# FP6 rounding in a macaron block: ScalarE makes the rounding constant and the half unit from the scaled values, VectorE drops its AND and, for activations, its OR

## What is computed

```python
def _nearest_on_grid(x, grid):                 # grid: all fp6 e2m3 values
    idx = jnp.clip(jnp.searchsorted(grid, x), 0, grid.shape[0] - 1)
    idx_lo = jnp.maximum(idx - 1, 0)
    v_hi, v_lo = grid[idx], grid[idx_lo]
    return jnp.where(jnp.abs(x - v_lo) <= jnp.abs(x - v_hi), v_lo, v_hi)

def _mx_quantize(t, eps=1e-30):                # blocks of 32 along a row
    blocks = t.reshape(rows, K // 32, 32)
    scales = jnp.maximum(jnp.max(jnp.abs(blocks), axis=-1) / 7.5, eps)
    return _nearest_on_grid(blocks / scales[..., None], _GRID), scales

# both the normed activations x2 and the weight w2 are quantized
out = xd @ wd.T + bias                          # xd = xq * xs, wd = wq * ws
x = x + 0.5 * _L1_ffn_ref(_layernorm(x), weight, bias)   # twice in the chain
```

## Time and profile before

| what | value |
|---|---|
| median of 3 runs | 2559.42 us (2553.13 to 2559.54) |
| span of the profiled execution | 2554.8 us (its page gives no other time of it; the median lies 4.6 us above) |
| instructions | 38679 |
| TensorE matmul busy | 2128.9 us, 83% of the span |
| VectorE busy | 1539.1 us, 60% |
| ScalarE busy | 970.2 us, 38% |
| GpSimd busy | 314.8 us, 12% |
| granted TensorE clock, mean | 0.903 of full |
| fourth stage (first `linear`) | about 1424 to 1644 us of the span |
| last stage (second `linear`) | about 2429 us to the end |

### The profile page before, as it was taken

One profiled execution on the slowest core, in us unless ns is written; L12 is line 12 of the kernel. 1 busy time (PEld: TensorE's weight loads), 2 busy tenths in 40 slices (PEclk: granted clock), 3 DMA queues, 4 the chain that ended last, 5 costly groups with the idle time before them and its releaser, 6 DMA issues.

```text
span 2554.8 us, 38679 instructions
## 1 busy us (share of the span) xinstructions
PE 2128.9 (83%) x12842; PEld 1592.0 (62%) x12842; DVE 1539.1 (60%) x4444; ACT 970.2 (38%) x1961; POOL 314.8 (12%) x298
## 2 busy tenths in 40 slices
PE   4589999957999956899999456578998998999846
PEld 2478888856788935788888335434445545555435
DVE  7744343446455577434343598576876776778287
ACT  4122232322333342232323334235556556555532
POOL 4320000031000044100000432311002002000000
PEclk8699999978999978999999657579999999999956
DMA  8110111020000031110110310422422422422001
GB/s 260 43 64 24 31 30 31 26 64 26 1 1 1 1 116 58 51 31 27 29 30 26 91 44 25 73 46 58 51 28 51 74 29 54 72 29 27 2 25 50
DMA packets 84036, 114.84 MB, mean 45 GB/s; under 512 B 12212, under 2 KB 73816, under 8 KB 80728
## 3 DMA queue, kind: packets, MB, share of 16 engines
q1 hardware_dynamic: 77416, 94.80, 17.0%
q0 software_dynamic: 6432, 17.57, 2.2%
HBM read 69.16 MB, written 43.17 MB: 44 GB/s over the span
## 4 chain that ended last, share of the span: by engine, by line
PE 61%; DVE 26%; ACT 5%; issue 4%; DMA 2%; POOL 2%; DVEq 0%; ACTq 0%; SPq 0%; POOLq 0%
PE psum L775 10%; PE psum L777 10%; PE psum L776 10%; PE psum L126 5%; PE psum L2298 4%; PE psum L128 4%; PE psum L127 4%; DVE mt L2186 3%; PE psum L2277 3%; PE psum L862 3%; DVE m L2174 2%; PE psum L2257 2%; DVE stats L160 2%; DVE m L2183 2%; DVE xn L185 2%
## 5 line engine op out<-in xcount | busy, mean ns | idle before, releaser
L2137 ACT ACTIVATE pt<-psum 128x512 f32<-128x512 f32 (+3 forms) x768 | 333.9, 492 | 274.9 <-DVE psum L2212 180.1
L740 DVE SCALAR_TENSOR_TENSOR h<-psum,xg,sg 128x128 f32<-128x128 f32 x592 | 166.7, 344 | 415.6 <-PE psum L862 415.6
L556 ACT ACTIVATE sg<-psum 128x512 f32<-128x512 f32 x180 | 107.7, 598 | 575.1 <-PE psum L777 575.1
L775 PE MATMUL psum<-w_hi,xt_hi 128*128 (+1 forms) x720 | 285.6, 397 | 33.7 <-DVE xt_lo L705 33.7
L776 PE MATMUL psum<-w_lo,xt_hi 128*128 (+1 forms) x720 | 283.8, 394 | 0.0
L777 PE MATMUL psum<-w_hi,xt_lo 128*128 (+1 forms) x720 | 283.7, 394 | 0.0
L2257 PE MATMUL psum<-ks,qs 96*128 96x512 bf16 (+3 forms) x768 | 235.5, 347 | 36.0 <-DVE m L2174 10.2
L2277 PE MATMUL psum<-qs,ks 99*128 99x512 bf16 (+3 forms) x768 | 239.0, 334 | 24.4 <-ACT pt L2137 18.8
L775 PE MATMUL psum<-w_hi,ht_hi 128*128 (+1 forms) x720 | 218.1, 303 | 0.2
L2186 DVE CUSTOM_DVE_ANT_0 mt<-psum,band_q 128x256 bf16<-128x256 f32 (+1 forms) x512 | 204.2, 399 | 18.3 <-PE psum L2257 8.1
L2281 PE MATMUL psum<-band,ident_r 128*128 128x256 f32 (+1 forms) x864 | 214.8, 337 | 0.0
(11 more groups left out here) (284 smaller groups left out, 4420.1 us busy)
## 6 DMA issues: line engine op xcount, KB each, us to landing
xg<-w_dram SPq DMA_DIRECT2D x54, 256.0 KB, 3.2
qk_scr<-parts SPq DMA_DIRECT2D x32, 384.0 KB, 2.5
qs<-qk_scr SPq DMA_DIRECT2D x96, 128.0 KB, 7.2
ks<-qk_scr SPq DMA_DIRECT2D x96, 128.0 KB, 7.8
xg<-rows_in SPq DMA_DIRECT2D x74, 132.0 KB, 2.1
rows_out<-yb SPq DMA_DIRECT2D x74, 128.0 KB, 1.7
x<-x_dram SPq DMA_DIRECT2D x4, 1024.0 KB, 8.6
out_dram<-x SPq DMA_DIRECT2D x4, 1024.0 KB, 4.5
```

The source lines that it names most:

```text
L740: ins = dve.scalar_tensor_tensor(out=h[i % 2][:, e, :], in0=u[:, e, :], scalar=xg[j % XSLOT][:, at:at + 1], in1=sg[i % 2][:, e, :], op0=AL ...
L775: pe.matmul(out, a[0], b[0], start=first, stop=False)
L2137: act.activation(pt[n % NPT][:, 0:q1 - q0], st_bank(n)[:, 0:q1 - q0], ACT.Exp).then_inc(*exped.up())
```

## The change

The `power` step of VectorE goes. A new step `sizes` on ScalarE waits for `scaled` and makes both helper tiles straight from the scaled values: `ulp` is |v| x 2^-24 for activations (a Relu, so zero for negative values, for the weight) and `e` is |v| x 2^20. The OR (`last_bit`) stays for the weight only. `less` waits for both new activations (before: for the first of its pair), and `shift` for `less` alone. The step list of a quad is one shorter, and `shift`, `even` and `requant` stand one place nearer to `less`, so steps that met in one round before meet in another now.

```diff
@@ weights()
-                for kind in ("scaled", "power", "less", "last_bit", "shift", "even", "requant"):
+                for kind in ("scaled", "sizes", "less", "last_bit", "shift", "even", "requant"):
@@ quad(d)
-                for kind in ("centre", "amax", "scaled", "power", "", "less", "last_bit", "shift", "even", "requant", ""):
+                for kind in ("centre", "amax", "scaled", "sizes", "", "less", "shift", "even", "requant", ""):
@@ on_act
-                        elif kind == "power":
-                            act.wait_ge(*power_ok(c + first))
+                        elif kind == "sizes":
+                            act.wait_ge(*scaled_ok(c + first))
                             if c - QUADS + first > 0:
-                                act.wait_ge(*less_ok(c - QUADS + first))
-                            act.activation(of(c).ulp, of(c).e, ACT.Relu, scale=2.0 ** -23).then_inc(*ulp_ok.up())
-                            act.activation(of(c).e, of(c).e, ACT.Abs, scale=ROUND).then_inc(*at_least.up())
+                                act.wait_ge(*even_ok(c - QUADS + first))
+                            act.activation(of(c).ulp, of(c).v, ACT.Abs if c >= 0 else ACT.Relu, scale=2.0 ** -24)
+                            act.activation(of(c).e, of(c).v, ACT.Abs, scale=2.0 ** 20).then_inc(*sized_ok.up())
@@ on_dve
-                        elif kind == "power":
-
-                            dve.wait_ge(*scaled_ok(c + first))
-                            dve.tensor_scalar(q.e.bitcast(U32), q.v.bitcast(U32), 0xFF800000, None,
-                                              ALU.bitwise_and).then_inc(*power_ok.up())
                         elif kind == "less":
-
-
-                            dve.wait_ge(*ulp_ok(c + first))
-
+                            dve.wait_ge(*sized_ok(c + first))
                             dve.tensor_tensor(q.v, q.ulp, q.v, ALU.subtract).then_inc(*less_ok.up())
@@
                         elif kind == "shift":
-                            dve.wait_ge(*at_least(c + first))
-                            dve.wait_ge(*no_tie(c + first))
+                            dve.wait_ge(*(less_ok(c + first) if c >= 0 else no_tie(1)))
```

More of the change, by code:

```diff
@@ L1283, in linear @@
             summed = S("summed")
-            centred, scaled_ok, power_ok, ulp_ok, less_ok, even_ok, quant_ok = (S(x) for x in (
-                "centred", "scaled", "power", "shift", "odd", "even", "requant"))
+            centred, scaled_ok, sized_ok, less_ok, even_ok, quant_ok = (S(x) for x in (
+                "centred", "scaled", "sized", "odd", "even", "requant"))
             turned, xt_hi, xt_lo, lin, lin_x = (S(x) for x in ("x_turned", "x_hi", "x_lo", "lin", "lin_x"))
             w_turned, wt_hi, wt_lo = S("w_turned"), S("wt_hi"), S("wt_lo")
-            first, at_least, no_tie = 1 if final else 2, S("at_least_one"), S("least")
+            first, no_tie = 1 if final else 2, S("least")
             def emptied(use):
@@ L1424, in on_dve @@
                             part.on_dve(kind, c, ring)
-                        q = of(c) if kind in ("amax", "scaled", "power", "less", "last_bit", "shift", "even", "requant") else None
+                        q = of(c) if kind in ("amax", "scaled", "less", "last_bit", "shift", "even", "requant") else None
                         if kind == "combine":
```

## The result

| | before | after |
|---|---|---|
| median | 2559.42 us (2553.13 to 2562.80, 5 runs) | 2517.44 us (2511.65 to 2527.38, 5 runs) |
| ratio, 95% interval | | 0.9841 (0.9822 to 0.9859) |
| span of the profiled execution | 2554.8 us | 2509.8 us |
| granted clock, mean | 0.903 | 0.916 |

The change is faster by 42 us where 27 were forecast: 2517.44 lies 1.6 us under the low end of the range. Two later sets of five runs of the same kernel gave medians of 2522.91 and 2519.15; the median of all fifteen is 2519.15, 40 us under before and just inside the range. So it is chance that the first five lie outside the range's low end (2519); that the gain is 13 to 15 us larger than forecast is not.

The account below looks back on a forecast made before the run. The prediction took a chain through VectorE and TensorE, with `lin` at 1.2 GHz, to bound both linear stages. Last stage 17.7 plus fourth stage 9.3 made 27 us, taking 2559.4 to 2532 us, range 2519 to 2543.

Parts of the forecast that it names:

- The loop: Both linear stages: sum, less, OR, amax, low, lin chain through VectorE and TensorE; last-stage period 14.02 us becomes 11.06.
- VectorE's 10.5: Last stage: VectorE's own work per period after the change, 10.5 us, the next bound behind TensorE's 11.06.
- The last stage's start: Before the last stage's first `low`: two ANDs and two ORs go, one `amax` moves behind; 4.3 us gained.
- ScalarE's covers: ScalarE's two activations per quad and `centre` just hidden behind VectorE work; priced at nothing, 0.3 to 0.5 us a quad otherwise.
- Up to the first `norm`: Fourth stage: five ANDs and five ORs go, `low` and `shift` come in front, wait shrinks; `norm` 5.2 us earlier.
- The six periods: Last stage, first to seventh quad's `low`: 81.8 us becomes 66.4, 15.4 saved.
- rival 2: Both linear stages: TensorE gets more 2.4 GHz, VectorE's 10.5 us sets the period; 37 us gained, 2522; chance 0.17.
- The 2 us given back at the end: Last stage's end: the last two quads' `lin` may lose their 2.4 GHz; 2 us taken, 6.0 with 1.2 GHz throughout.
- the term behind the second `norm`: Fourth stage: second projection copied 24.3 us behind the `norm` instead of 28.4, stage end 4.1 earlier; bounds 0 and 8.
- Between the `norm`s: Fourth stage: earlier first projection against a second one behind `lin`; net -1.9 to +2.1 us, taken as 0.
- The first (only removed work counts, 2540): Both stages: new order brings nothing, at most 19.4 us gained, 2540; with a same-time variant (2541), chance 0.19.
- The third (slower, `lin` in front): Both stages: period stays 14.0, two `lin` groups in front of projections cost 8.2 us each; 2571; chance 0.03.

Follow-up runs that it names:

- Work only: The changed instructions in the old step order, an empty step where the OR's was, so `amax` stays in front of `low`: 2536.27 us (0.9909).
- order only: The kernel before, AND and OR kept, in the new step order with `amax` behind `low`: 2539.45 us (0.9919).
- the stage alone: The change in the fourth stage only, the last stage keeping AND, OR and the old order: 2545.32 us (0.9952).
- full fillers: Useless 128-row matmuls in front of `lin`: kernel before 2544.03 us; changed kernel 2516.26, and with more, also at the head projection, 2509.88.
- The first filler runs: Extra 2-row bias matmuls in front of `lin` pairs: eight in the kernel before, 2561.58 us; two to 12 in the changed kernel, 2523.59.

## Why the prediction was short

**Right.** The loop, and what it is worth at 1.2 GHz. The period was to be 11.06 us and is 10.99 where the clock stays low; VectorE's 10.5 is 10.38; `low` was to come 1.8 us behind the second `sum` and comes 1.74. The last stage's start was to gain 4.3 us and gains 4.4. Work only and order only gave the two periods that the same reasoning yields, 13.30 and 11.73. ScalarE's covers held in the periods; only at the stage's start, where no `sum`s stand in between, does `less` wait:

```profile
2417.30 1.22 DVE L1460 TENSOR_TENSOR centred<-ulp,centred 128x1024 f32<-128x1024 f32 x1 [2.07 <-ACT power L1404]
```

Up to the first `norm` 5.2 us were forecast, and 5.2, 7.2 and 5.1 measured.

**Last stage, 17.7 forecast, 23.7, 17.9 and 19.6 in three traces.** Here a size was off. The six periods were put at 66.4 us, all at 1.2 GHz, and take 64.2, 64.7 and 64.3: some of them reach VectorE's limit, as rival 2 had it for all. The 2 us given back at the end (seventh `low` to last `sum`) were 1.7 won in the first trace and 3.5 and 2.2 given back in the others.

**Fourth stage, 9.3 forecast, 19.7, 18.1 and 18.9 in three traces, 12.4 in the median of the stage alone.** This is the step that failed, and above all the term behind the second `norm`, "4.1 more. Bounds 0 (POOL or ScalarE later than before) and 8". It measured 12.6, 8.5 and 12.2, and 9.3 in the trace of the stage alone: over the upper bound all four times. By its own parts, for the first trace:

- "the transposes' ScalarE input comes after 8.4 us, as before": 6.6. POOL's add is 1.75 us shorter, because one two-source instruction stands behind the `norm` and then `sum` and the statistics, where `even`, the AND and `requant` stood. I had priced the AND on VectorE's own queue alone.
- "There `lin` now starts (8.18), and both projections follow (2.8 each)": 5.5 and 1.4 each, 5.5 us less, by the clock. In the second trace only 1.4 of this came, in the second projection.
- "That one feeds the awaited transfer, so the stage's end moves with it": from the second copy to the last `low` it takes 9.1 us and not 11.0, since the transposes' `xt_hi` is now issued in front of the fourth copy, the one that waited for the second transfer. 1.9 us.

Together 1.75 + 5.5 + 1.9 = 9.1, less 0.8 from TensorE's end to the copy, which I had left out: 8.3 on top of 4.1 is 12.4, and 12.6 was measured. Between the `norm`s 0 was forecast and 1.9 came, its best bound, although POOL's first add took 3.2 us longer: the clock again rose before the second projection. In other executions of like kernels it did not, and that stretch took 48.7 to 48.9.

The bounds failed with the sum. They left out the shared port, and of the two levels of the clock they gave the faster one to `lin` alone and not to the projections behind it. That the stage alone shows 12.4 in the median, and 13.6 in its trace, where the traces of the whole change show 18 to 20, stays open. In that trace the stage's mean clock is 0.61 where the first trace has 0.66. The intervals of the two halves just reach the whole, so it may be chance or it may be that the stages act on each other; no run tells these apart.

**Rivals.** The first (only removed work counts, 2540) falls with the run of the order alone. The second (2522) had the time nearly right, for half the reason: TensorE did get more of 2.4 GHz, but in stretches that differ from run to run. Whether the shorter idle time brought it is not shown: filled with 2-row matmuls to 122 of 127 us the stage stayed at 0.53; with 128-row ones it rose to 0.81. The third (slower, `lin` in front) shows in the order-only kernel between the `norm`s, where 3.9 us are lost and the second copy comes 30.65 us behind the first `norm` in place of 23.67; it is outweighed. With the rule that the second rival quotes from the Trainium skill (TensorE: Matmul & The Clock Gate, section What's actually happening), that activity releases the throttle, the full matmuls agree; the thin ones do not, though the profile counts them as busy.

The Trainium skill, SBUF — State Buffer, section Who interferes with whom, states that VectorE with two SBUF inputs, or in a 2-port mode, and a GpSimd instruction that reads SBUF exclude each other. The trace agrees to 0.1 us (5.02, 3.27, 2.36). By that rule the add's 5.02 would have been read as 2.35 and three VectorE instructions, and the AND's removal as 0.6 us more on the projection's path.

A version with a second pair of `parts` slots, which might free the third copy of its wait of 2.78 us, wasn't tried.

## What to carry to other kernels

Where two engines hand a loop back and forth, write the loop as a chain and ask of each instruction whether it stands between the hand-overs or beside them: moving one step of five instructions (`amax`) out of the chain paid about as much here (20 us) as removing 32 instructions (23 us). Price a removed or moved instruction also on the engine that shares its port, in both directions. And where stretches like `lin` run at 1.2 GHz, forecast both levels per stretch, not per stage, since one program lands on different ones from run to run. The fifteen runs of the changed kernel span 16 us, and the long ones have the lower mean clock (2511.65 us at 0.916, 2527.38 at 0.908), but full fillers, which raised the clock, did not narrow the spread.

## What the runs showed of the hardware

- Matmuls with 2 rows kept TensorE busy 122 of 127 us and left the granted clock at 0.53; 20 matmuls of 128 rows in each of the same places brought it from 0.61 to 0.81, and a kernel with nothing but such useless work added got 14.6 us faster.
- POOL's add waits through a whole series of VectorE instructions that follow each other without a gap, not only through the one that was running: 2.35 us alone, 3.27 behind one, 5.02 behind even, AND and `requant`. In the one place seen where a gap of 0.03 us stands between two of them, POOL gets in and VectorE waits: its `requant` then takes 3.27 us in place of 1.22.
- An AND on one source, 0.68 us long, holds POOL up as a two-source instruction does: 3.89 against 3.27.
- Matmuls of 256 columns follow each other every 0.21 us at 1.2 GHz and every 0.12 at 2.4, though the profile gives each 0.41 and 0.28 (and the bias ones 0.58 and 0.38). The first filler runs were mispriced for taking the longer figure.
